# Adding the first layer's second bias to the tokens on GpSimd instead of in TensorE's product

## What is computed

```python
def layer(x):
    x = x + gnn(layernorm(x))
    return x + ffn(layernorm(x))

def gnn(x):
    agg = epsilon * x + adjacency @ x            # within a block of 256 tokens
    h = silu(rmsnorm(agg @ W1 + b1, rms_weight)) # W1: 128 x 512
    return h @ W2 + b2                           # W2: 512 x 128; b2: the bias of this change

def ffn(x):
    xn = layernorm(x) * gamma + beta
    w = softmax of the two largest of xn @ Wr + br, over 8 experts
    return sum over the two chosen experts of w * (gelu(xn @ W1[e] + b1[e]) @ W2[e] + b2[e])
```

## Time and profile before

| | us |
|---|---|
| median of 3 runs | 447.06 (445.47 to 447.8) |
| the profiled execution | 446.49 |
| its span, first to last instruction | 444.7 |
| PE busy | 402.4 (90% of the span) |
| DVE, ACT, POOL busy | 298.2, 281.7, 298.1 |

### The profile page before, as it was taken

How to read it: one execution, slowest core, us unless ns; L and a number is a source line. 1 busy time by engine, 2 the same in 40 slices (tenths; PEclk the granted TensorE clock), 3 DMA queues, 4 the chain that set the end, 5 groups by cost and what they waited for, 6 DMA issues and landing times.

```text
span 444.7 us, 11925 instructions
## 1 busy us (share of the span) xinstructions
PE 402.4 (90%) x2932; PEld 349.0 (78%) x2932; DVE 298.2 (67%) x1267; ACT 281.7 (63%) x652; POOL 298.1 (67%) x445
## 2 busy tenths in 40 slices
PE   0899999999999999998879986799999899999993
PEld 0567777777777878776779875699989898999993
DVE  4597877889887888967744561266566666755652
ACT  1278776777677778777785543366676776545540
POOL 1233568787777888887781678766656566777775
PEclk9999999999999999999999999689999999999998
DMA  6879873233332231111165155455555453331110
GB/s 181 257 228 313 295 215 105 65 99 107 110 119 78 81 110 39 50 49 40 61 177 133 57 132 152 139 138 146 135 150 148 123 135 104 102 98 37 36 38 31
DMA packets 41175, 53.51 MB, mean 120 GB/s; under 512 B 5842, under 2 KB 35794, under 8 KB 40468
## 3 DMA queue, kind: packets, MB, share of 16 engines
q1 hardware_dynamic: 33040, 32.95, 27.3%
q0 software_dynamic: 6096, 18.52, 11.8%
q10 hardware_dynamic: 1972, 1.28, 1.1%
HBM read 38.01 MB, written 22.31 MB: 136 GB/s over the span
## 4 chain that ended last, share of the span: by engine, by line
PE 64%; DVE 11%; issue 11%; DVEq 7%; DMA 2%; ACT 1%; another core or an unknown queue 1%; POOL 1%; ACTq 0%; POOLq 0%
PE banks L810 12%; PE banks L793 11%; PE banks L627 10%; PE banks L650 10%; PE banks L615 6%; PE banks L636 5%; PE banks L672 3%; DVEq L1504 2%; DVEq L1525 2%; PE banks L773 2%; PE banks L662 2%; DVE result L1532 1%; DVEq L1532 1%; DVE hidden L1082 1%; DVEq L1518 1%
## 5 line engine op out<-in xcount | busy, mean ns | idle before, releaser
L561 POOL DMA_INDIRECT out<-result,rows_in x92 | 90.1, 979 | 54.0 <-DVE result L1532 48.6
L810 PE MATMUL banks<-w_sb,hidden_e 128*128 (+1 forms) x736 | 105.5, 285 | 6.1 <-DVE result L1532 4.8
L810 PEld LDWEIGHTS banks<-w_sb,hidden_e 128*128 128x128 f32 x736 | 93.5, 195 | 9.2 <-issue 8.5
L946 ACT ACTIVATE hidden_e<-banks 128x512 f32<-128x512 f32 x92 | 54.9, 597 | 49.5 <-PE banks L793 39.3
L505 POOL DMA_INDIRECT rows_dram<-rows_out,row_of x64 | 67.9, 1061 | 23.4 <-issue 10.8
L627 PE MATMUL banks<-gw_sb,agg 128*128 128x512 f32 x128 | 67.3, 611 | 0.9 <-DVE gw_sb L983 0.9
L650 PE MATMUL banks<-gw_sb,hidden_t 128*128 128x128 f32 x512 | 67.6, 275 | 0.0
L650 PEld LDWEIGHTS banks<-gw_sb,hidden_t 128*128 128x128 f32 x512 | 63.5, 192 | 0.8
L858 ACT ACTIVATE hidden<-banks 128x512 f32<-128x512 f32 x64 | 38.2, 597 | 30.4 <-PE banks L627 27.3
L636 PEld LDWEIGHTS banks<-fixed,hidden 128*128 128x128 f32 x256 | 30.5, 141 | 34.4 <-issue 29.7
L940 ACT ACTIVATE xg_t<-banks,ones 128x128 f32<-128x128 f32 x92 | 33.5, 364 | 33.1 <-PE banks L773 19.9
(11 more groups left out here) (147 smaller groups left out, 765.0 us busy)
## 6 DMA issues: line engine op xcount, KB each, us to landing
rows_in<-rows_dram SPq DMA_DIRECT2D x92, 132.5 KB
adj<-adj_t SPq DMA_DIRECT2D x16, 512.0 KB, 4.9
x_tok<-x SPq DMA_DIRECT2D x16, 256.0 KB, 4.0
rows_dram<-idle_in POOLq DMA_DIRECT2D x1, 3710.0 KB
rows_dram<-idle_in SPq DMA_DIRECT2D x28, 132.5 KB
out<-result,rows_in POOLq DMA_INDIRECT x92
w_sb<-w SPq DMA_DIRECT2D x1, 1024.0 KB, 6.3
b_bc<-b SPq DMA_DIRECT2D x1, 1024.0 KB, 10.7
```

The lines of the kernel that those rows point to most:

```text
L561: nc.gpsimd.indirect_dma_start(out=out, out_offset=bass.IndirectOffsetOnAxis(ap=rows_in[:, i % RING][:, IDX_AT:IDX_AT + 1].bitcast(U32), a ...
L810: last = pe.matmul(y_ps(i)[:, w], hidden_e[:, i % 4, w * HCE + c], w2_sb[:, bass.ds(at + c * D, D)], start=(c == 0 and i >= EARLY), stop=( ...
L946: nc.scalar.activation(hidden_e[:, i % 4], h_ps(i), ACT.Gelu).then_inc(gelu_done, 1)
```

## The change

GpSimd adds b2, held once in all partitions, to the group's tokens in place, after `normalise1` has read them and three steps before `residual` adds them to the product. It does so in step g+1, in POOL's order where `leave_space()` stood; in steps 17 and 18, which have no such group, `leave_space()` stays. The product on PE, its operands, `prep_bias` and one DVE fill go; the first product of each tile now starts the accumulation itself; the two one-row loads become one load to all partitions. `residual` waits for `x_biased` too.

```diff
-        bias_loads = [
-            (bias_raw[0:1], gb2_wide), (bias_raw[32:33], gb2_wide),
-        ]
+        bias_loads = [(gb2_bc[:], gb2.partition_broadcast(P))]
@@ GpSimd
+            def add_bias(g):
+                if g == 0:
+                    pool.wait_ge(bias_in, BIAS)
+                pool.wait_ge(xn1_ready, g + 1)
+                nc.gpsimd.tensor_tensor(x_tok[:, g % XR], x_tok[:, g % XR],
+                                        gb2_bc[:].unsqueeze(1).to_broadcast([P, TPG, D]), ALU.add
+                                        ).then_inc(x_biased, 1)
+
             for s in range(STEPS):
                 if g6 is not None:
                     send_rows(g6, 0)
                 if g4 is not None:
                     put_tokens(g4)
+                if g1 is not None:
+                    add_bias(g1)
+                elif g6 is not None:
+                    leave_space()
                 if g6 is not None:
-                    leave_space()
                     send_rows(g6, 1)
@@ TensorE, narrow
                         pe.wait_ge(consts_in, CONSTS)
-                        pe.wait_ge(bias_ready, 1)
-                    pe.matmul(z_ps, bias_sel[:], bias2_parts[:], start=True, stop=True)
                 for c in range(HC1):
                     last = pe.matmul(z_ps[:, t * P:(t + 1) * P], hidden_t[:, g % 2, c, t * P:(t + 1) * P], gw2_sb[:, c],
-                                     start=False, stop=True, skip_group_check=True)
+                                     start=(c == 0), stop=(c == HC1 - 1))
@@ VectorE
-                nc.vector.memset(bias_sel[:].bitcast(F32), 0.0)
-                nc.vector.memset(bias2_parts[:].bitcast(F32), 0.0).then_inc(fills_done, 1)
+                nc.vector.memset(bias_sel[:].bitcast(F32), 0.0).then_inc(fills_done, 1)
-            def prep_bias():
-                ... 
             def residual(g):
                 dve.wait_ge(z_done, g + 1)
+                dve.wait_ge(x_biased, g + 1)
@@ VectorE, step 3
-                    prep_bias()
                     prep_rank()
```

## The result

| | us |
|---|---|
| median before, run beside it | 446.99 (445.47 to 447.80, 4 runs) |
| median after | 453.44 (449.59 to 455.52, 4 runs) |
| after / before | 1.014 (95% interval 1.0072 to 1.0208) |
| profiled execution, before and after | 446.49 and 449.59 |
| step 18's rank product on PE starts, before and after | 220.53 and 224.24 |

The change makes the kernel slower by 1.4%; 446.7 us with a range of 444.4 to 449.8 was forecast. To find the mechanism I use the start of PE's rank product in each step (L687 in the kernel after, L681 in the kernel before). It lies in the first phase, and the length from step 5's to step 18's leaves out the start of the program as well.

A forecast was written before the change was run, and what follows sets the result against it. PE and DVE were taken to bound the first phase by turns. Gains of 1.41 us less costs of 1.09 gave -0.32: 446.49 - 0.3 = 446.2 us profiled, 446.7 against the median, range 444.4 to 449.8.

The forecast's parts named there:

- wait list of PE: First phase, PE: the chain of waits and the slack before L681; removing the bias product gains 1.83 us together.
- folding steps: Steps 7 to 10, where the chain goes over ACT and DVE's folding to `chosen`; removing the product gains nothing.
- -1.83: First phase: the whole gain from removing sixteen bias products on PE, 1.83 us, before the add's costs.
- The add's price: GpSimd's add in steps 6 to 16: two streams sharing a port, 1.04 us, 0.66 longer than the memset.
- lower end: GpSimd's add counted as one stream only: 0.20 + 0.42 = 0.62 us.
- The mechanism: DVE operations with two SBUF inputs held up by POOL's reading add; steps 7, 13, 14, 15 net 1.09 us longer.
- lay 1.04 us over the memset's place: First phase: a 1.04 us window at the memset's old times, delaying the next two-input DVE operation, such as L1129 or L1131.
- The covers: Load, `residual`'s wait for `x_biased`, and POOL's work queued behind the add up to `scale2`: counted 0.
- near 12: The b2 load to all partitions, before `scale1` of step 1: would land near 12 us, counted 0.
- The slower one: Rival: an add of 1.6 us or more reaches DVE's two-input operations from step 7 on; +3.1 us, 450.2; chance 0.12.
- The rival without hold-up: Rival: DVE hardly held up by the add, so 1.83 us stay; 444.7 profiled, 445.2 median; chance 0.18.
- The clock: Rival: PE's granted clock, 0.82 over 276 to 304 us, drops or doubles its loss; 442 or 452; chance 0.12.

The follow-up runs named there:

- copy of 512: After with the add replaced by a copy of the group's tokens onto themselves (128x512, one input), no b2 added: 447.31 us, one run.
- fill of the same length: After with the add replaced by a memset of 128x1340 that reads nothing, same waits, no b2 added: 447.89 us, ratio 0.9988.
- run with the wait: After with POOL waiting for its own copy of four columns (put_tokens) to complete before the add: 434.64 us, one run.
- half add: After with the add over two of the four tiles only (128x256), the other two without b2: 447.77 us, one run.
- three adds: After with b2 added for groups 7, 11 and 13 alone (steps 8, 12, 14), the memset in the other steps: 430.52 us, one run.
- add and product: Before with PE's bias product kept and a GpSimd add of zeros in the memset's place, residual waiting for it: 453.87 us, ratio 1.0107.
- after again: After, unchanged, timed again beside before on another chip, granted clock 0.995: 436.45 us against 431.18, ratio 1.0135.
- timed run: After with the add waiting for put_tokens to complete, timed on a third chip: 449.85 us against 447.81, ratio 1.0046.

## Why the prediction was wrong, point by point

**The wait list of PE, right.** The slack said that steps 6, 11, 13 and 16 gain 0.235 us, step 14 0.18, and step 12, 15, 17 and the folding steps nothing. Without the add, steps 6, 11, 13 and 16 came out shorter by 0.23 or 0.24, step 14 by 0.17, step 12 and the folding steps by 0.00 or 0.01, as the earlier trace rows had said; steps 15 and 17 stayed within 0.02. Step 18 gained 0.21 where nothing was expected. Up to step 5 the phase is 1.19 us earlier, where 0.7 was expected. The rest is in the start of the program; it varies between runs (step 5's rank product starts between 53.65 and 54.56 in the kernels without the bias product), and I can't say how much of it belongs to the change. So -1.83 became -2.50.

**The add's price, too low.** I took 1.04 from streams of 0.21 us for 256 columns. One stream was priced right: the copy of 512 took 0.62, and my lower end had been 0.62. Two were not: from 128x256 (0.73 to 0.79) to 128x512 (1.27) it is 0.5 for 256 columns, not 0.42, and about 0.2 is fixed. The estimate from the GPSIMD Engine Reference of the Trainium skill, 1.12, was nearer and still short. The prediction said that the result turns above an add of about 1.2 us; it was 1.27. That alone makes little of the loss, as the first point below shows.

**The mechanism, right where it was named; its price, 6.3 us instead of 1.5.** The add's reading holds up DVE operations with two SBUF inputs: the fill of the same length, inside which they keep their length, shows it. L1087, with a PSUM input, is untouched, and so are the TENSOR_REDUCE `top` (0.18 us inside the add in steps 8 to 11) and the BATCH_NORM_STATS2 (0.28 inside the add in step 13 of the run with the wait), with one SBUF input each. One SBUF input isn't enough to be safe, though: the TENSOR_SCALAR `neg_mean` is held by the add, by the half add (0.43 us in step 16) and by the write-only fill. The prediction didn't have this; in after itself `neg_mean` meets no add in steps 5 to 18, so it has no share in the loss.

The arithmetic from hold to loss was right too. In step 13 the hold is 1.70 - 0.19 = 1.51, less the 0.185 of slack that is left there: 1.33, measured 1.32. In steps 12, 14 and 15 it is 1.08, 1.37 and 1.39, measured 1.10, 1.38 and 1.38; in step 16, with 1.44, it is hidden, as expected. What failed is the term "lay 1.04 us over the memset's place", in three ways:

1. Its length. The hold ends 0.05 to 0.07 us after the add's end, so it is 1.33 us behind the add's start. With before's distances this gives 0.4 us for step 7 and, in steps 13 to 15, 0.7, 0.5 and 0.5, or 2.1 in all, instead of 1.5: 0.6 us of the 4.8 that were missing. That the holder keeps the pair of ports for the whole instruction is what the Trainium skill says (SBUF — State Buffer, section Who interferes with whom; it says so of DVE's two-port modes, and calls the pair an exclusive lock in general). I had weighed it at 0.1 us a step, against a row of before that showed a delay of only 0.16. The runs agree with the page, and so did that row; I had misread it. A `score` of 0.19 us that is held ends 0.06 us behind the add, which is its own length less 0.13. L1220, 0.97 us long, should then end 0.84 behind the copy's end at 257.44, at 258.28, and it did. Where the two met again, without the add, with three adds, and with add and product, it was 0.84, 0.84 and 0.83. Nor was L1220 alone in the row with 0.97, though that is its undisturbed length: POOL's `scale2` (L471), 0.20 us in the steps up to 16, started inside it and was held to 0.06 us behind its end.

```profile
207.68 0.84 POOL L471 TENSOR_TENSOR shift<-neg_mean,rstd 128x4 f32<-128x4 f32 x1
```

So the trace of before showed the whole hold in both directions.

2. Its beginning. I took DVE operations that start before the window for free; the first `score` of steps 13 to 15, and of step 7, starts 0.2 to 0.35 us before the add's shown start and was held all through. That is where most of the loss is: these four steps lost 4.6 of the 6.3 us, steps 13 to 15 alone 4.1. One wait, on POOL's own copy in front of the add, frees these operations and takes back 3.4 us on the same chip. Why the hold begins early is open (below).

3. Its place. The windows were laid over the timeline of before, as if the change did not move it. Each hold makes DVE late against POOL's sends or the other way round; the distance from the add's start to the first `score` fell from 0.84 (memset, before) to 0.31 us in steps 8 to 11, and from 1.19 to 0.06 in step 12, which I had put down as free. The kernel with three adds shows step 12 at 0.31 us with its neighbours gone, and at 1.10 with them.

The three don't add up by themselves, since each moves the others. With the wait in place, the add costs 2.7 and 3.5 us in two runs; without the wait, 6.1 to 6.3.

**The covers, right.** The load landed before POOL needed it: POOL's 5.6 us of idle time ended at 12.86 us, where "near 12" stood. `residual` waited for nothing: the fill has the same wait and loses nothing. The same holds for `scale2`: POOL's longer step is covered.

**The rivals.** The slower one named a wrong threshold more than a wrong mechanism: it asked for an add of 1.6 us, put "clearly slower" at 1.5 and gave 450.2, which is +3.1 us; at 1.27 us the medians differ by 6.4. It priced step 13 at 0.97, and steps 14 and 15 at 0.77 and 0.95, which is still under what was measured, for want of the second and third point. The rival without hold-up is refuted. The clock is no part of the inner length, by the granted clock of 1.00 over the first 225 us of both profiles, and the ratio stays in the run with a clock of 0.995.

**What stays open.** The ends of the first phases differ by 3.7 us between the two profiles, and the profiled executions by 3.10; the medians of the first comparison by 6.4, and on the other chip by 5.3. The part above 3.7 lies behind the first phase. One piece can be seen: from the rank product of step 18 to that of step 19 the profiles show 17.6 to 18.0 us or 19.1 to 19.6, and not by kernel (before 17.6, after 19.2, after again 17.8). In the second phase the order of the rows, POOL's scatter and the reads from memory meet, and executions of the kernel before on one chip lay between 445.57 and 452.23. I didn't separate it.

## What to carry to other kernels

Before an operation is moved to GpSimd, look at whether it reads SBUF and at what DVE does beside it. In this kernel a reading operation of full length was a hole in DVE's schedule for operations with two SBUF inputs, and the price was that length at the place where it fell, less DVE's slack there, however short the DVE operation was. A TENSOR_SCALAR with one SBUF input fell into the same hole, even beside a write-only fill. DVE work that reads PSUM, TENSOR_REDUCE and BATCH_NORM_STATS2 ran beside the add at their usual lengths. Here a place 1.1 us earlier in step 13, and over 2 us earlier against `score` in steps 8 to 11, cost 1.3 us instead of 6.3. And a place that a write-only filler holds at no cost says nothing of what a reading operation costs there.

## What the runs showed that had not been expected

The hold begins before the profile shows the add to begin. In after it is up to 0.35 us ahead, in the kernel with both the add and the product 0.67, through a copy of four columns and part of an indirect DMA in front of it. Every operation that was held from 0.18 us ahead or more had started while POOL's indirect DMA in front of the copy was still shown. With a wait for the copy's completion, `score` operations that started inside that DMA kept their 0.19 us, one of them 0.50 us ahead of the copy (step 13 of the timed run), where the kernel with the add and the product held one from 0.51 ahead.

The GPSIMD Engine Reference of the Trainium skill (section 2.1, Instruction dispatch) says that each of GpSimd's cores starts the next instruction as soon as it is done with its own share of the one before. That would fit the long holds: an early core could begin to read while the record still shows the predecessor, and a wait on completion would stop it. It doesn't by itself explain why a half add and a copy, issued behind the same predecessors without a wait, let a `score` through that started as far ahead. The trace has no row for single cores. So what is shown is the early hold with the full add and its end with the wait; the cause stays open.
